# Forty unread products on TensorE around the first counts of a graph-layer kernel

## The chip, the cores and the metric

The kernel runs on one core of a Trainium2 chip. The core has five engines that run their own instruction streams and meet at semaphores: TensorE (PE, matrix products, with PEld for its weight loads), VectorE (DVE), ScalarE (ACT), GpSimd (POOL) and SyncE (SP, which issues transfers). The metric is the device time of one execution in microseconds. The time of a kernel is the median of several executions.

## The reference

One layer of a graph network over 6250 nodes with 64 features and 206250 edges sorted by destination:

```python
h = jnp.maximum(_layernorm(x, axis=-1), 0.0)
msg = h[src] + edge_attr_64
agg = jax.ops.segment_sum(msg, dst, num_segments=6250)
x = x + (jax.nn.relu(agg @ W1 + b1) @ W2 + b2)
```

## The kernel before

The 6250 nodes are 49 tiles of 128, handled as 25 double tiles of 256 (DTS = 25, LAST = 24; the last is half empty). The gather h[src] is not done row by row. For each double tile the kernel builds a table of counts, how often each source node feeds each destination node of the double tile, and multiplies it by h. So per double tile there are these steps:

- *Slots.* POOL gathers for each destination node up to 64 edge codes from a table in memory (gather_slots, L509, tile ell). The address comes from row pointers that DVE works out (L647), and those need another gather of POOL (gather_rows, L489, tile g).
- *Match and turn.* DVE marks foreign slots (match, L661, tile hi_m). PE transposes the codes (turn_codes, L805 and L806), ACT copies them out of PSUM (codes, L372).
- *Hots.* DVE writes one-hot tables lo_hot and hi_hot from the codes, in five batches (hots, L675), into two buffers. A batch waits until the counts of the batch two before it are done.
- *Counts.* PE multiplies lo_hot by hi_hot, 50 or 52 small products for each batch, in three thirds (count, L831). ACT copies each third from PSUM into the table (copy_counts, L407). A third waits for the copy of the third three before it.
- *Sums.* h is held as three bf16 parts. PE multiplies the table by two parts at once (high_sums, L844, 49 products of 256 columns) and by the third (low_sums, L852, 49 products), and adds the edge features with small f32 products (edge_sums, L866). All land in one PSUM bank, sum_ps.
- *Layer.* The sums go through W1, relu and W2 (hidden L881, rows L888), DVE adds x, SP stores.

PE's order is written out by hand. In pass j of its loop it runs rounds v = 0 to 4; in each it does batch v of the counts of double tile j, then a part of the sums of double tile m = j - 1, and at v = 2 the transposes for double tile j + 1 and turn_rel (L816, positions of edges) for j. HIGH and LOW say which part of the sums a round takes:

```python
HIGH = [0, 20, 20, 40, 40, 49]
LOW = [0, 0, 5, 5, 17, 49]
```

So pass 0 has counts and transposes alone, with nothing to sum yet. The first sums, 20 of them, stand behind the counts of batch 0 of pass 1. They wait for all copies of double tile 0. DVE and POOL run ahead of PE: at the time of pass 1's third round DVE matches double tile 2, whose slots POOL gathered before.

Of the kernel before, what the change touches and what calls it, by code (L numbers as in the profile page):

```python
# [6 lines left out]
def build_gnn_layer(nc, x, src, dst, edge, w1, b1, w2, b2, out):  # L7
# [6 lines left out]
    P = 128  # L14
# [45 lines left out]
    def steps_of(j):  # L60
        return 3 * batches_of(j)

    def step_index(j, u):
        return STEPS * j + u
# [10 lines left out]
    def tiles_in(j):  # L75
        return 2 if j < LAST else 1
# [11 lines left out]
    with ctx:  # L88
        def sb(name, shape, dt=f32):
            return ctx.enter_context(nc.sbuf_tensor(name, shape, dt))  # L90

        def ps(name, shape, dt=f32):
            return ctx.enter_context(nc.psum_tensor(name, shape, dt))

        def sem(name):
            return ctx.enter_context(nc.semaphore(name))
# [62 lines left out]
        ones_b = sb("ones_b", [P, P], bf16)  # L159
# [3 lines left out]
        ident_b = sb("ident_b", [P, P], bf16)  # L163
# [30 lines left out]
        sum_ps = [ps(f"sum_ps{b}", [P, 512]) for b in range(2)]  # L194
# [4 lines left out]
        def out_ps(f):  # L199
            return sum_ps[f % 2][:, 2 * P:2 * P + 2 * F]  # L200
# [4 lines left out]
        def rel_ps(j):  # L205
            return sum_ps[j % 2][:, 0:KK * 2 * CK]
# [26 lines left out]
        matched, turned, codes_made = sem("matched"), sem("turned"), sem("codes_made")  # L233
# [14 lines left out]
        with nc.Block() as block:  # L248
# [538 lines left out]
            def _(pe):  # L787
                pe.wait_ge(first_made, 1)
                for k in range(PR):
                    nc.tensor.matmul(row_ps, l_hot[:, k * P:(k + 1) * P], a_eq[:, k * HI:k * HI + NT],  # L790
                                     start=(k == 0), stop=False, skip_group_check=True)
                for k in range(PR):
                    last = nc.tensor.matmul(row_ps, ones_b[0:ROWP, :], a_lt[:, k * HI:k * HI + NT],
                                            start=False, stop=(k == PR - 1), skip_group_check=True)
# [13 lines left out]
                def turn_rel(j):  # L808
                    n = tiles_in(j) * CK
                    pe.wait_ge(rel_made, j + 1)  # L810
                    if j >= 1:
                        pe.wait_ge(rel_copied, j)
                    if j >= 2:
                        pe.wait_ge(rows_added, j - 1)
                    for k in range(KK):
                        last = nc.tensor.transpose(rel_ps(j)[:, k * 2 * CK:k * 2 * CK + n],  # L816
                                                   rel_rows[j % 2][0:n, k:CHUNK:KK], ident[0:n, 0:n])
                    last.then_inc(rel_turned, 1)

                def count(j, u):  # L820
                    g = step_index(j, u)
                    n = batch_index(j, u // 3)
                    if u % 3 == 0:
                        pe.wait_ge(hots_made, n + 1)
                    if g >= 3:
                        pe.wait_ge(copied, g - 2)
                    a, b = step_pairs(j, u)
                    for i in range(b - a):
                        for h in range(2):
                            rows = slice(h * SLOTS, (h + 1) * SLOTS)  # L830
                            last = nc.tensor.matmul(count_ps[u % 3][:, h, i * NT:(i + 1) * NT],  # L831
                                                    lo_hot[n % 2][rows, a + i, :], hi_hot[n % 2][rows, a + i, 0:NT],
                                                    start=True, stop=True)
                    last.then_inc(counted, 1)
# [6 lines left out]
                def high_sums(m, his):  # L841
                    cols = sum_cols(m)
                    for s in his:
                        nc.tensor.matmul(sum_ps[m % 2][:, 0:cols], parts[:, s, 0:2 * F],  # L844
                                         counts[m % 2][:, s, 0:cols], start=(s == 0), stop=False,
                                         skip_group_check=True)
# [29 lines left out]
                def hidden(f):  # L876
                    cols = 2 * P if f < LAST else 2 * HALF
                    pe.wait_ge(agg_copied, f + 1)
                    if f >= 1:
                        pe.wait_ge(rows_added, f)  # L880
                    nc.tensor.matmul(hid_ps(f)[:, 0:cols], w1_sb[:, :], agg_sb[:, 0:cols],  # L881
                                     start=True, stop=True).then_inc(hid_made, 1)

                def rows(f):
                    pe.wait_ge(relu_made, f + 1)
                    for h in range(tiles_in(f)):
                        n = P if f < LAST else NLAST
                        last = nc.tensor.matmul(out_ps(f)[0:n, h * F:(h + 1) * F], hid_sb[:, h * P:h * P + n], w2_sb[:, :],  # L888
                                                start=True, stop=True)
                    last.then_inc(rows_made, 1)  # L890

                HIGH = [0, 20, 20, 40, 40, 49]
                LOW = [0, 0, 5, 5, 17, 49]
                assert HIGH[-1] == NT and LOW[-1] == NT

                turn_codes(0)
                for j in range(DTS + 1):
                    m, f = j - 1, j - 2
                    for v in range(ROUNDS):
                        for u in range(3 * v, 3 * v + 3):  # L900
                            if j < DTS and u < steps_of(j):
                                count(j, u)
                        if f >= 0 and v == 0:
                            if f == 0:
                                pe.wait_ge(w_in, 80)
                            hidden(f)
                        if f >= 0 and v == 1:
                            rows(f)
                        if m >= 0:
                            if v == 0:  # L910
                                pe.wait_ge(copied, step_index(m, 0) + steps_of(m))
                                pe.wait_ge(rel_copied, m + 1)
                                pe.wait_ge(codes_made, min(m + 2, DTS))
                                if m == 0:
                                    pe.wait_ge(part_made, 2)
                                    pe.wait_ge(rest_in_parts, 1)
                                if m >= 2:
                                    pe.wait_ge(agg_copied, m - 1)
                                if m == LAST - 2:
                                    pe.wait_ge(shift_made, 1)  # L920
                                if m == LAST:
                                    pe.wait_ge(far_read, 1)
                            high_sums(m, range(HIGH[v], HIGH[v + 1]))
                            if v % 2 == 1 and v // 2 < tiles_in(m):
                                edge_sums(m, v // 2, range(TILES_E))
                            if LOW[v] < LOW[v + 1]:
                                last = low_sums(m, range(LOW[v], LOW[v + 1]))
                            if v == ROUNDS - 1:
                                last.then_inc(sums_done, 1)
                        if v == 2 and j + 1 < DTS:  # L930
                            turn_codes(j + 1)
                        if v == 2 and j < DTS:
                            turn_rel(j)
                        if j == LAST - 2 and v == 3:
                            pe.wait_ge(rp_made, DTS)
                            pe.wait_ge(codes_made, LAST)
                            pe.wait_ge(rel_copied, LAST - 1)
                            nc.tensor.matmul(shift_ps[0:P - HALF, :], ident[:, HALF:P], rp_f[:, NT - 1:NT],
                                             start=True, stop=True).then_inc(shifted, 1)
                        if j == LAST and v == 3:  # L940
                            pe.wait_ge(r0_set, LAST)
                            pe.wait_ge(rel_copied, DTS)
                            nc.tensor.matmul(next_ps, next_a, rp_f[:, 0:NT], start=True, stop=False)
                            nc.tensor.matmul(next_ps, next_b, rp_f[:, 1:NT + 1], start=False, stop=True)
                            nc.tensor.matmul(base_ps, ones[0:1, 0:P], r0_f[0:1, :], start=True, stop=True
                                             ).then_inc(far_found, 1)
                        if j == DTS and v == 2:
                            pe.wait_ge(worst_made, 1)
                            pe.wait_ge(rows_added, DTS - 1)
                            nc.tensor.transpose(worst_ps[0:1, :], worst[:, 0:1], ident).then_inc(worst_turned, 1)  # L950
# [167 lines left out]
```

## Time and profile before

| | us |
|---|---|
| median of 3 runs | 521.38 |
| lowest, highest | 519.58, 523.01 |
| the profiled execution | 519.95 |
| its span, first to last instruction | 518.2 |

| engine | busy us | share of the span | instructions |
|---|---|---|---|
| PE | 459.3 | 89% | 12541 |
| PEld | 405.9 | 78% | 12541 |
| DVE | 435.2 | 84% | 531 |
| ACT | 380.2 | 73% | 481 |
| POOL | 322.5 | 62% | 223 |

How to read it: the busy share is an average over stages. The first 50 us build tables and have little work for PE. The page also gives the TensorE clock granted over the span, on average 0.992 of full speed. The chain of waits follows the work that ended last back from the end, each step to what released it. A group of instructions in a timeline is merged, and a pause ahead of it stands in brackets with its releaser.

### The profile page before, as it was taken

The page shows a single profiled execution, that of the slowest core. Times are in us where ns is not written, and L with a number is a line of the kernel's source. Part 1 is how long each engine was busy: PE and PEld are TensorE (multiplying, and loading weights), DVE is VectorE, ACT ScalarE, POOL GpSimd, SP SyncE. Part 2 cuts the span into 40 slices and gives each one's busy share as a digit, 9 for nine tenths or more (in the row PEclk, how much of TensorE's full clock was granted, in tenths as well). Part 3 has the DMA queues.
Part 4 walks back from the last instruction along what each step waited for, and adds up shares of the span by engine and source line. Part 5 has one row for each costly group of instructions (what it writes and reads, how often), then busy time and mean ns, then how long its engine had stood idle before and what let it go on. Part 6 is the DMA issues. An engine that isn't in the chain of part 4 may idle for free.

```text
span 518.2 us, 27591 instructions
## 1 busy us (share of the span) xinstructions
PE 459.3 (89%) x12541; PEld 405.9 (78%) x12541; DVE 435.2 (84%) x531; ACT 380.2 (73%) x481; POOL 322.5 (62%) x223
## 2 busy tenths in 40 slices
PE   1012799999999999999999999999999999999994
PEld 1002688898889888888888988988898898888883
DVE  4989977988988998998898899889889988969550
ACT  2846766787878787787878878878787887878720
POOL 4379998976676566657756666756757675125200
PEclk9999989999999999999999999999999999999997
DMA  9758057643663474466357346536744643661200
GB/s 203 186 142 259 19 145 198 203 133 111 185 187 103 141 200 121 114 187 171 97 159 201 107 126 193 150 94 178 195 108 130 198 131 99 185 182 51 78 3 10
DMA packets 139626, 73.65 MB, mean 142 GB/s; under 512 B 23644, under 2 KB 137550, under 8 KB 139382
## 3 DMA queue, kind: packets, MB, share of 16 engines
q1 hardware_dynamic: 136105, 65.30, 45.8%
q0 software_dynamic: 3168, 4.90, 3.5%
q8 instruction: 100, 1.64, 1.2%
q10 hardware_dynamic: 234, 1.65, 1.0%
q14 instruction: 19, 0.16, 0.1%
HBM read 66.98 MB, written 4.86 MB: 139 GB/s over the span
## 4 chain that ended last, share of the span: by engine, by line
PE 84%; POOL 6%; DMA 3%; ACT 2%; DVE 2%; issue 1%; SPq 0%; ACTq 0%; DVEq 0%; POOLq 0%
PE sum_ps L844 25%; PE sum_ps L866 21%; PE count_ps L831 17%; PE sum_ps L852 14%; POOL ell L509 3%; PE sum_ps L881 3%; PE sum_ps L888 3%; POOL g L489 2%; DMA comb_rows<-counts 1%; PE sum_ps L816 1%; DMA dst_sb<-in_dst 1%; DMA ell<-comb_rows,ell_idx 1%; ACT counts L343 1%; ACT counts L345 1%; POOL r_f L496 1%
## 5 line engine op out<-in xcount | busy, mean ns | idle before, releaser
L407 ACT CAST counts<-count_ps 128x882 bf16<-128x882 f32 (+2 forms) x369 | 327.0, 978 | 60.2 <-PE count_ps L831 59.1
L675 DVE TENSOR_TENSOR lo_hot<-iota_lo,codes 128x3328 bf16<-128x3328 bf16 (+3 forms) x123 | 229.9, 1869 | 41.3 <-PE count_ps L831 25.0
L509 POOL DMA_INDIRECT ell<-comb_rows,ell_idx x50 | 105.2, 2103 | 90.2 <-DVE ell_idx L647 56.5
L844 PE MATMUL sum_ps<-counts,h_parts 128*128 128x256 bf16 (+1 forms) x1225 | 145.4, 273 | 0.0
L844 PEld LDWEIGHTS sum_ps<-counts,h_parts 128*128 128x128 bf16 x1225 | 114.5, 99 | 18.2
L831 PE MATMUL count_ps<-hi_hot,lo_hot 64*128 64x49 bf16 x6256 | 110.4, 183 | 16.8 <-DVE hi_hot L675 14.8
L831 PEld LDWEIGHTS count_ps<-hi_hot,lo_hot 64*128 64x128 bf16 x6256 | 96.0, 94 | 37.3 <-DVE hi_hot L675 19.6
L489 POOL DMA_INDIRECT g<-in_dst,row_i x49 | 95.5, 1949 | 37.9 <-DVE e_hot L689 21.3
L866 PE MATMUL sum_ps<-e_hot,edges 128*64 128x24 f32 x3528 | 112.9, 217 | 1.0 <-issue 1.0
L866 PEld LDWEIGHTS sum_ps<-e_hot,edges 128*64 128x64 f32 x3528 | 107.7, 138 | 3.7 <-issue 1.1
L675 DVE TENSOR_TENSOR hi_hot<-iota_hi,codes 128x1300 bf16<-128x1300 bf16 (+3 forms) x123 | 103.9, 844 | 0.0
L852 PE MATMUL sum_ps<-counts,h_parts 128*64 128x256 bf16 (+1 forms) x1225 | 81.1, 273 | 0.3 <-issue 0.3
L852 PEld LDWEIGHTS sum_ps<-counts,h_parts 128*64 128x64 bf16 x1225 | 62.0, 111 | 6.1 <-issue 5.7
L520 POOL TENSOR_SCALAR rel_rows<-dst_rows,tile_base 36x256 f32<-36x256 int32 (+1 forms) x25 | 47.7, 1910 | 24.3 <-DMA dst_rows<-in_dst 23.4
L689 DVE TENSOR_TENSOR e_hot<-win_tab,rel_sb 128x864 f32<-128x864 f32 x49 | 53.0, 1081 | 5.7 <-ACT rel_sb L381 5.7
L390 ACT COPY agg_sb<-sum_ps 128x256 f32<-128x256 f32 (+1 forms) x25 | 9.2, 367 | 36.3 <-PE sum_ps L852 36.3
L528 POOL TENSOR_TENSOR x_sb<-x_sb,b_all 128x128 f32<-128x128 f32 (+1 forms) x25 | 28.2, 1130 | 1.6
L805 PE MATMUL sum_ps<-ident_b,ell 128*128 128x128 bf16 x25 | 5.6, 224 | 21.7 <-DVE hi_m L661 21.7
L499 POOL CAST r_i<-r_f 1x2 int32<-1x2 f32 x24 | 22.9, 954 | 1.5
L805 PEld LDWEIGHTS sum_ps<-ident_b,ell 128*128 128x128 bf16 x25 | 2.8, 113 | 22.2 <-issue 19.3
L496 POOL TENSOR_SCALAR r_f<-rp_f 1x2 f32<-1x2 f32 x24 | 17.3, 722 | 2.5 <-DVE rp_f L649 1.9
L372 ACT COPY codes<-sum_ps 128x512 bf16<-128x512 bf16 x25 | 14.8, 593 | 5.4 <-PE sum_ps L806 5.4
(107 smaller groups left out, 213.7 us busy)
## 6 DMA issues: line engine op xcount, KB each, us to landing
edges<-in_edge_attr SPq DMA_DIRECT2D x98, 576.0 KB, 5.2
h_rows<-h_sb SPq DMA_DIRECT2D x1, 1568.0 KB, 10.3
x_sb<-in_x SPq DMA_DIRECT2D x4, 384.0 KB, 10.2
out<-o_sb SPq DMA_DIRECT2D x24, 64.0 KB, 1.7
comb_rows<-counts ACTq DMA_DIRECT2D x1, 1443.8 KB
dst_rows<-in_dst SPq DMA_DIRECT2D x49, 18.0 KB
ell<-comb_rows,ell_idx POOLq DMA_INDIRECT x50
g<-in_dst,row_i POOLq DMA_INDIRECT x49, 4.0
```

The lines of the kernel that those rows point to most:

```text
L407: nc.scalar.copy(counts[j % 2][:, :, 0:2 * half].rearrange("p s (h i) -> p h s i", h=2)[:, :, :, first + a:first + b], count_ps[u % 3][:, ...
L489: nc.gpsimd.indirect_dma_start(out=g2[j % 2][:, h, :], out_offset=None, in_=dst.rearrange("(r e) -> r e", e=STEP), in_offset=bass.Indirect ...
L499: nc.gpsimd.tensor_copy(r0_i[0:1, 2 * j:2 * j + n], r0_f[0:1, 2 * j:2 * j + n]).then_inc(r0_made, 1)
L509: nc.gpsimd.indirect_dma_start(out=ell[j % 2][0:rows, h, :, :].rearrange("p s w -> p (s w)"), out_offset=None, in_=comb_dram[:, :], in_off ...
L520: nc.gpsimd.tensor_scalar(rel_rows[j % 2][0:n * CK, :], dst_rows[j % 2][0:n * CK, :], float(2 * j * P), tile_base[0:n * CK, 0:1], ALU.subt ...
L528: nc.gpsimd.tensor_tensor(x_sb[:, tiles, :], x_sb[:, tiles, :], bc(b2_all[:, :].rearrange("p (o f) -> p o f", o=1), [P, tiles_in(f), F]), ...
L675: return nc.vector.tensor_tensor(out_ap.rearrange("p i (a t) -> p i a t", t=2), bc(table_ap.rearrange("p (o a t) -> p o a t", o=1, t=2), [ ...
L689: nc.vector.tensor_tensor(e_hot[h][:, :, :].rearrange("p (c k) w -> p c k w", k=KK), bc(win_tab[:, m // LAST, :, :].rearrange("p c (o w) - ...
L831: last = nc.tensor.matmul(count_ps[u % 3][:, h, i * NT:(i + 1) * NT], lo_hot[n % 2][rows, a + i, :], hi_hot[n % 2][rows, a + i, 0:NT], sta ...
L844: nc.tensor.matmul(sum_ps[m % 2][:, 0:cols], parts[:, s, 0:2 * F], counts[m % 2][:, s, 0:cols], start=(s == 0), stop=False, skip_group_che ...
L852: last = nc.tensor.matmul(sum_ps[m % 2][half, 0:cols], parts[:, s, 2 * F:3 * F], counts[m % 2][:, s, 0:cols], start=False, stop=False, ski ...
L866: last = nc.tensor.matmul(sum_ps[m % 2][half, low:low + W], edges[t % SLOT_EDGES][:, c, k * F:(k + 1) * F], e_hot[h][:, i, :], start=False ...
```

## The change

A helper keep_busy issues a number of products of the identity (ident_b, the weights) with a table of ones (ones_b, 128 columns) into the first 128 columns of sum_ps[1]. Nobody reads them. The next user of this bank starts with start=True. In pass 0 ten such products follow the work of each of the rounds 2, 3 and 4, behind a wait for codes_made of at least 1 (ACT's copy of double tile 0's codes, which read the same bank). In pass 1 ten more stand in round 0, between the counts and the first sums. All other engines' instructions stay as they were.

```diff
+                def keep_busy(times):
+                    for _ in range(times):
+                        nc.tensor.matmul(sum_ps[1][:, 0:P], ident_b[:, :], ones_b[:, :], start=True, stop=True)
+
                 HIGH = [0, 20, 20, 40, 40, 49]
                 LOW = [0, 0, 5, 5, 17, 49]
                 assert HIGH[-1] == NT and LOW[-1] == NT
@@ -906,6 +910,8 @@
                             hidden(f)
                         if f >= 0 and v == 1:
                             rows(f)
+                        if j == 1 and v == 0:
+                            keep_busy(10)
                         if m >= 0:
                             if v == 0:
                                 pe.wait_ge(copied, step_index(m, 0) + steps_of(m))
@@ -931,6 +937,9 @@
                             turn_codes(j + 1)
                         if v == 2 and j < DTS:
                             turn_rel(j)
+                        if j == 0 and v >= 2:
+                            pe.wait_ge(codes_made, 1)
+                            keep_busy(10)
```

PE's order before, from the transposes of pass 0 to the first sums of pass 1 (count_ps0 to count_ps2 are the three thirds of a batch, and hi_hot0 and hi_hot1 the two buffers of hots):

```order
L816 MATMUL sum_ps0<-wide,rel_rows0 128x36 x2
L831 MATMUL count_ps0<-hi_hot1,lo_hot1 128x49 x18
L831 MATMUL count_ps1<-hi_hot1,lo_hot1 128x49 x16
L831 MATMUL count_ps2<-hi_hot1,lo_hot1 128x49 x16
L831 MATMUL count_ps0<-hi_hot0,lo_hot0 128x49 x18
L831 MATMUL count_ps1<-hi_hot0,lo_hot0 128x49 x16
L831 MATMUL count_ps2<-hi_hot0,lo_hot0 128x49 x16
L831 MATMUL count_ps0<-hi_hot1,lo_hot1 128x49 x18
L831 MATMUL count_ps1<-hi_hot1,lo_hot1 128x49 x18
L831 MATMUL count_ps2<-hi_hot1,lo_hot1 128x49 x16
L844 MATMUL sum_ps0<-counts0,h_parts 128x256 x20
```

The same place in the changed kernel, from the transposes to the second group of new products (L894 is the new line):

```order
L816 MATMUL sum_ps0<-wide,rel_rows0 128x36 x2
L894 MATMUL sum_ps1<-ones_b,ident_b 128x128 x10
L831 MATMUL count_ps0<-hi_hot1,lo_hot1 128x49 x18
L831 MATMUL count_ps1<-hi_hot1,lo_hot1 128x49 x16
L831 MATMUL count_ps2<-hi_hot1,lo_hot1 128x49 x16
L894 MATMUL sum_ps1<-ones_b,ident_b 128x128 x10
```

And from there, behind the last counts of pass 0, to the first sums of pass 1:

```order
L831 MATMUL count_ps2<-hi_hot0,lo_hot0 128x49 x16
L894 MATMUL sum_ps1<-ones_b,ident_b 128x128 x10
L831 MATMUL count_ps0<-hi_hot1,lo_hot1 128x49 x18
L831 MATMUL count_ps1<-hi_hot1,lo_hot1 128x49 x18
L831 MATMUL count_ps2<-hi_hot1,lo_hot1 128x49 x16
L894 MATMUL sum_ps1<-ones_b,ident_b 128x128 x10
L844 MATMUL sum_ps0<-counts0,h_parts 128x256 x20
```

Nothing changed its place among the old instructions; four groups of ten stand between them, one ahead of each of the three batches of counts and one ahead of the sums.

## Rows read from the trace of the kernel before

**Rows 1.** The page, chain that ended last: shares of the span by engine.
```profile
PE 84%; POOL 6%; DMA 3%; ACT 2%; DVE 2%; issue 1%; SPq 0%; ACTq 0%; DVEq 0%; POOLq 0%
```

**Rows 2.** Chain of waits, 26 to 85 us: start, duration, what.
```profile
50.13 12.38 POOL ell L509
...
62.81 4.54 DMA ell<-comb_rows,ell_idx
...
69.74 0.73 DVE hi_hot L675
```

**Rows 3.** PE's waits, 49 to 79.4 us, then 79.4 to 490: total, times, longest.
```profile
PE count_ps L831 <- DVE hi_hot L675: 4.6, 4, 1.8
```
```profile
PE count_ps L831 <- issue: 1.4, 2, 0.9
```

**Rows 4.** Timeline of PE, 0 to 80 us: start, duration, instructions, pause before.
```profile
49.78 0.45 PE L816 MATMUL sum_ps<-wide,rel_rows 36*128 36x36 f32 x2
52.05 1.22 PE L831 MATMUL count_ps<-hi_hot,lo_hot 64*128 64x49 bf16 x50 [1.82 <-DVE hi_hot L675]
54.51 0.89 PE L831 MATMUL count_ps<-hi_hot,lo_hot 64*128 64x49 bf16 x34 [1.23 <-DVE hi_hot L675]
55.87 0.52 PE L831 MATMUL count_ps<-hi_hot,lo_hot 64*128 64x49 bf16 x16 [0.47 <-ACT counts L407]
57.06 1.58 PE L831 MATMUL count_ps<-hi_hot,lo_hot 64*128 64x49 bf16 x52 [0.67 <-DVE hi_hot L675]
58.57 4.18 PE L844 MATMUL sum_ps<-counts,h_parts 128*128 128x256 bf16 x20
62.68 0.84 PE L831 MATMUL count_ps<-hi_hot,lo_hot 64*128 64x49 bf16 x52
...
66.76 2.36 PE L844 MATMUL sum_ps<-counts,h_parts 128*128 128x256 bf16 x20
...
69.16 0.43 PE L816 MATMUL sum_ps<-wide,rel_rows 36*128 36x36 f32 x2
70.52 0.81 PE L831 MATMUL count_ps<-hi_hot,lo_hot 64*128 64x49 bf16 x50 [0.93 <-DVE hi_hot L675]
71.26 2.98 PE L866 MATMUL sum_ps<-e_hot,edges 128*64 128x24 f32 x72
...
79.35 0.81 PE L831 MATMUL count_ps<-hi_hot,lo_hot 64*128 64x49 bf16 x50
```

**Rows 5.** Timeline of all engines, 30 to 80 us, rows of ACT and DVE.
```profile
52.65 8.02 ACT L407 CAST counts<-count_ps 128x882 bf16<-128x882 f32 x9 [0.50 <-PE count_ps L831]
...
61.93 1.88 DVE L675 TENSOR_TENSOR lo_hot<-iota_lo,codes 128x3328 bf16<-128x3328 bf16 x1
...
67.38 0.48 DVE L661 SCALAR_TENSOR_TENSOR hi_m<-ell,node_f 128x64 bf16<-128x64 f32 x2 [2.82 <-DMA ell<-comb_rows,ell_idx]
...
67.92 1.82 DVE L675 TENSOR_TENSOR lo_hot<-iota_lo,codes 128x3200 bf16<-128x3200 bf16 x1
```

**Rows 6.** Busy time by microsecond; the third number from the end is PE's clock.
```profile
72.00:73.00 1.00, 1.00 (x36) 1.00 (x32) 1.00 (x3) 1.00 (x3) 1.00 (x1) 0.79 0.37 108
73.00:74.00 1.00, 1.00 (x24) 1.00 (x24) 1.00 (x1) 1.00 (x2) 1.00 (x1) 0.50 0.00 1
...
76.00:77.00 1.00, 1.00 (x40) 0.90 (x35) 0.85 (x2) 0.94 (x2) 1.00 (x1) 1.00 0.61 170
...
86.00:87.00 1.00, 0.43 (x15) 0.42 (x16) 0.01 (x1) 0.00 (x0) 0.95 (x1) 1.00 0.36 82
```

**Rows 7.** Timeline of PE, 76 to 200 us.
```profile
86.57 1.18 PE L866 MATMUL sum_ps<-e_hot,edges 128*64 128x24 f32 x35 [1.05 <-issue]
...
128.74 0.22 PE L831 MATMUL count_ps<-hi_hot,lo_hot 64*128 64x49 bf16 x2
...
129.72 2.29 PE L866 MATMUL sum_ps<-e_hot,edges 128*64 128x24 f32 x72
...
136.31 0.84 PE L831 MATMUL count_ps<-hi_hot,lo_hot 64*128 64x49 bf16 x52
```

## The prediction

> **What bounds the kernel now.** I read the page's chain shares first: TensorE (PE) holds 84% of the chain that ended last, POOL 6% and DMA 3% [rows 1]. So PE is the bound over most of the span, but not everywhere, and the change sits in the part where I must know which. The second view is the chain of waits around the edit, 50 to 71 us. There it does not run on PE. It runs through a POOL gather of slots that takes 12.38 us from 50.13, the landing of that double tile's gathers (4.54 us from 62.81) and then DVE's match and one-hots, the last of which ends at 70.47 [rows 2]. Only after that, with the counts at 70.52, does the chain enter PE. The third view is PE's waits: from 49 to 79.4 us it waited 4.6 us for DVE's hi_hot; from 79.4 to 490 us it waited for no engine at all, the largest entry being 1.4 us of "issue" [rows 3]. The reader is to see two regimes: up to 70.5 us PE is fed late by POOL, DMA and DVE and has slack; from 70.5 us on every microsecond that PE loses or wins stays to the end.
>
> The fourth view is PE's timeline through the edit [rows 4]. Counts of 50 or 52 products take 1.22 to 1.26 us at first, 0.81 to 0.84 later. The first 20 high sums take 4.18 us at 58.57, the next 20 take 2.36 us at 66.76. That is a factor of nearly two on the same shapes, so PE ran at 1.2 GHz until about 62.5 us and at 2.4 GHz after. (The granted-clock column reads 1.00 there already; I go by the durations.) Later the column does show a fall: 0.79 in the microsecond from 72, 0.50 from 73, 1.00 again from 76 [rows 6]. If the fraction of the first is split between the two levels, the clock fell at 72.6. Ahead of that fall PE had stood still for 0.93 us, from 69.59 to 70.52, waiting for hi_hot [rows 4].
>
> **What the change adds.** Forty products of 128x128 by 128 columns in four groups of ten, each with its weight load: one group after the transposes of double tile 0's round 2, one after its round 3, one after its round 4, and one between the first counts of double tile 1 and the first sums. Nothing is removed or moved. The three groups in double tile 0 wait for codes_made of 1, and ACT had to raise that before any hot could be made, long ago; these waits are free.
>
> Price of one product: half of a 256-column sum. At 1.2 GHz 4.18 us over 20 is 209 ns, so 105 ns each and 1.05 us a group. At 2.4 GHz 2.36 us over 20 is 118 ns, so 59 ns each and 0.59 us a group [rows 4]. All forty cost 2.4 to 4.2 us of PE. The Trainium skill, in "TensorE: Matmul & The Clock Gate", section "Wait — 56ns, not 53.3ns?", has 107 and 56 ns for this width, and by it the forty would cost 2.2 to 4.3 us; the trace agrees within 6%.
>
> Where they lie, at the dear price. *Group 1* starts when the transposes end at 50.23 and ends at 51.28; the next counts began at 52.05, released by DVE: hidden. *Group 2* starts at 53.27 and ends at 54.32; the next counts began at 54.51: hidden, with 0.2 us to spare. *Group 3* starts at 56.39 and ends at 57.44; counts began at 57.06, so they are 0.38 us late. These 52 counts took 1.58 us to the sums' start, where others of 52 take 1.26, since the last third waited for ACT's copy. Without a pause they now end at 57.44 + 1.26 = 58.7 instead of 58.57. *Group 4* is uncovered: 1.05 us, so the sums start at 59.8 instead of 58.57 [rows 4]. Who would notice? Behind these products on PE stand the counts, and DVE waits for the counts two batches back before it refills a buffer. Its lo_hot at 61.93 and 67.92 need counts that ended at 58.57 and 63.5: each has over 3 us of margin, and DVE shows no idle before the 2.82 us in which it waits for the gathered slots at 67.38 [rows 5]. ACT copies without a gap from 52.65 to 60.67, nine copies, so the last of them, which takes the late counts, starts only near 59.8 [rows 5]. So nothing on the POOL, DMA and DVE chain moves. If the cover were gone, all forty would cost 2.4 to 4.2 us.
>
> What they bring. PE works more continuously from 50 to 59 us, and the clock can rise sooner than at 62.5. At best it is at 2.4 GHz when the sums start. Then they take 2.36 us instead of 4.18, the fourth group costs 0.59, and PE is done with the sums 4.18 - 2.36 - 0.59 = 1.2 us ahead of before. If the clock rises no sooner than before, (62.5 - 59.8) / 0.209 = 13 sums run slowly, the other 7 take 0.83, and PE is done at 63.35, 0.6 us later than before (62.75).
>
> **Where that goes.** Both end at the counts of 70.52. They need DVE's hi_hot, ready at 70.47, and PE was at that point at 69.59. PE 0.6 us later: still 0.3 us in time. PE 1.2 us earlier: it first waits for match at 67.86 to do the transposes, then for 70.47 [rows 2, 4, 5]. Direct term: 0 from both sides. The one term left is the clock with which PE goes into the stretch from 70.52, where it is the bound. From the counts at 70.52 to the first counts of the next double tile at 79.35 it took 8.83 us; the same stretch three double tiles on takes 7.57 us (128.74 to 136.31) at 2.4 GHz [rows 4, 7]. So the fall of 72.6 costs 1.26 us now. The changed kernel has it, has more of it, or has none of it. PE stands still between 69.59 and 70.52 now; after an early rise it would stand still for longer, up to 0.9 + 1.2 = 2.1 us. The only fall in the trace inside the work came right after such a pause, so the fall should stay, and may come sooner. Price of sooner: the counts of 70.52 at 1.22 instead of 0.81 us (0.41), and the edge sums. Their 72 products from 71.26 took 2.98 us with the fall inside [rows 4]. At the rate of the clean stretch (2.29 us for 72, 32 ns each [rows 7]) some 42 were done in the 1.34 us to 72.6, and the other 30 took 1.64 us, 55 ns each; all at 55 ns is 3.96, or 0.98 more. Together +1.4 us. I take 0 for this term as the likeliest, with ends of -1.26 and +1.4.
>
> The sum: profiled execution 519.95 us + 0 + 0 = 519.95. It lies 1.43 us under the median of the three runs, 521.38, whose span (519.58 to 523.01) is as wide as the ends of my term; so **521.4 us** for the median.
>
> A rule bears on this. The rows give the cold stretch as 57 to 62.5 us, some 1% of the span, and it cannot give more than half of that back, 2.8 us. The Trainium skill, same page, section "What's actually happening", says that the slow start costs under 1% of a typical kernel, and that the number of slow products at its start differs from run to run. By that rule too this change can't be measured at the 1% bound, and the rule says besides that one profile is no proof of where the clock rises.
>
> **Rivals.**
> 1. *The half clock comes sooner after the longer pause*: slower, the other side. Place: PE's counts and edge sums from 70.5; price +1.4 us, 522.8. It decides if PE's granted clock is at 0.50 when hi_hot lands. For: the fall of 72.6 followed a pause of 0.93 us, which the change can double. Against: PE also stood still for 1.05 us ahead of 86.57 ("issue") [rows 7] with no fall in the microsecond after [rows 6]. Chance 0.2.
> 2. *The fall goes away*: -1.26 us, 520.1. For: it came only once within the work, and what PE does before it moves. Against: the pause gets longer. Chance 0.15.
> 3. *The early gain goes through in full*, because the chain is on PE there after all: -1.2 us, 520.2. Against: the 0.93 us wait at 70.52 would have to be misread. Chance 0.03.
> 4. *The change doesn't do what it says*: the clock rises no sooner, and the fourth group delays the sums. The 0.6 us is within the slack, 521.4. Chance 0.1.
> 5. *Something larger*, such as the 12.38 us gather coming out another way: over 5.2 us either way. No row leads there from these products. Chance 0.05.
>
> **How the numbers follow.** The forecast (clock sooner, time the same) has the rest, 0.47. One per cent is 5.2 us, about what a measurement can tell from no change; cases 1 to 4 and the forecast all lie within it. Of case 5 I give 0.02 to faster and 0.03 to slower. The range takes the ends of the clock term (520.1 and 522.8) and some 1.1 us more on either side, since the median of before moved by 1.8 and 1.6 us between runs: 519.0 to 523.9. About 2 in 10 is left out.
>
> **What would show it.** Right: in the profile of the changed kernel the first 20 sums take 2.2 to 3 us instead of 4.18, PE's wait for hi_hot ahead of the counts near 70.5 grows from 0.93 to about 2 us, and those counts start within 0.3 us of 70.52. Wrong in the cover: DVE's hots or POOL's gather start later than at 61.93 and 62.81. Wrong in the clock term: the stretch from these counts to the next double tile's takes 7.6 us (fall gone) or 10.2 us (fall sooner) instead of 8.8. The whole prediction is wrong if the counts near 70.5 move by over 1 us, since then PE or the products touch the POOL and DVE chain.

## The result and the profile after

| | before | changed |
|---|---|---|
| median of 6 runs, us | 521.51 | 535.77 |
| lowest, highest | 519.58, 523.01 | 533.78, 538.62 |
| profiled execution | 519.95 | 538.62 |
| its span | 518.2 | 536.9 |

The changed kernel is slower by 2.8%: ratio 1.0279, 95% interval 1.0255 to 1.0303. The forecast of 521.4 us and its range of 519.0 to 523.9 missed it. Medians in this document are of all executions, ratios only of those within 1.5% of the fastest execution of the same kernel, so that a ratio can differ from the quotient of two medians.

Where PE's idle time went, from the view of waits of the changed kernel (line, waited for: us in total, times, longest):

```profile
PE count_ps L831 <- DVE hi_hot L675: 11.0, 5, 4.6
...
PE sum_ps L844 <- issue: 6.3, 4, 2.2
PE sum_ps L852 <- issue: 5.1, 8, 1.2
PE count_ps L831 <- issue: 4.6, 3, 2.0
...
PE sum_ps L866 <- issue: 0.3, 1, 0.3
```

"Issue" is idle time in which PE waited for no engine that the profile shows. It is 16.3 us here; before it was 2.7 us behind 79.4 us, with 1.4 us as the largest entry [rows 3].

PE's timeline of the changed kernel (start, duration, instructions, pause before) shows that this does not happen where the products were put, but later:

```profile
58.05 1.25 PE L894 MATMUL sum_ps<-ones_b,ident_b 128*128 128x128 bf16 x10
59.10 2.70 PE L844 MATMUL sum_ps<-counts,h_parts 128*128 128x256 bf16 x20
...
69.06 0.81 PE L831 MATMUL count_ps<-hi_hot,lo_hot 64*128 64x49 bf16 x50 [0.22 <-DVE hi_hot L675]
...
77.62 0.70 PE L881 MATMUL sum_ps<-agg_sb,w_sb 128*128 128x256 f32 x2
...
86.85 0.24 PE L831 MATMUL count_ps<-hi_hot,lo_hot 64*128 64x49 bf16 x5 [1.72 <-issue]
87.02 4.02 PE L844 MATMUL sum_ps<-counts,h_parts 128*128 128x256 bf16 x20
...
245.36 1.14 PE L852 MATMUL sum_ps<-counts,h_parts 128*64 128x256 bf16 x17 [0.45 <-issue]
...
321.67 1.58 PE L852 MATMUL sum_ps<-counts,h_parts 128*64 128x256 bf16 x25 [1.20 <-issue]
340.74 1.69 PE L852 MATMUL sum_ps<-counts,h_parts 128*64 128x256 bf16 x27 [0.66 <-issue]
...
437.44 0.70 PE L844 MATMUL sum_ps<-counts,h_parts 128*128 128x256 bf16 x5 [1.71 <-issue]
457.87 0.93 PE L844 MATMUL sum_ps<-counts,h_parts 128*128 128x256 bf16 x7 [2.24 <-issue]
...
529.13 0.47 PE L881 MATMUL sum_ps<-agg_sb,w_sb 128*128 128x112 f32 x2 [0.35 <-ACT agg_sb L390]
```

The first product with W1 (L881) stands at 77.62, where before it stood at 80.12:

```profile
80.12 0.70 PE L881 MATMUL sum_ps<-agg_sb,w_sb 128*128 128x256 f32 x2
...
510.29 0.47 PE L881 MATMUL sum_ps<-agg_sb,w_sb 128*128 128x112 f32 x2 [0.35 <-ACT agg_sb L390]
```

So at the end of the first double tile the changed kernel was 2.5 us ahead. The products in place are not what brought that: with 20 products far ahead of them and none in place (e6 below) the first L881 stands at 77.67 too. From the first to the last L881 the changed kernel took 451.5 us instead of 430.2: 21.3 us lost, all in the steady part, where both kernels have the same instructions. Pauses of kind issue are 13.3 us of it (16.0 in the changed kernel behind 77 us, 2.7 before). Three of them, of 1.72, 2.24 and 2.02 us, each go with a fall of PE's clock to 1.2 GHz at or soon after their end. For the first, the busy time by microsecond shows it (the third number from the end is the clock):

```profile
87.00:88.00 1.00, 1.00 (x10) 0.70 (x6) 0.80 (x1) 0.81 (x1) 0.97 (x2) 0.55 0.18 52
88.00:89.00 1.00, 1.00 (x7) 0.71 (x5) 1.00 (x2) 0.00 (x0) 1.00 (x1) 0.50 0.31 91
```

Twenty high sums took 4.02 us there instead of 2.36 [rows 4], 1.7 us more; three times that, some 5 us, is my estimate for the three falls. The other 3 us I can't book to single rows; low sums of 2.34 us instead of 1.94 behind 133 us are of that kind.

The rows also show a pattern. At each pause PE stands a given number of products short of the end of a group: 17, 25, 27 low sums, later 5, 7 high sums. That number grows by two per double tile. This looks as if something were counted off in PE's instruction stream.

**The theory, F.** PE's instructions come from memory in blocks. The page of the kernel before has them as a DMA queue (packets, MB, share of the engines):

```profile
q8 instruction: 100, 1.64, 1.2%
```

That is 100 transfers of 16 KB for 12541 products and as many weight loads, some 65 bytes an instruction, so some 250 instructions in a block. The pattern above fits 256, or 128 products with their loads. A double tile has 508 such products by PE's timeline, and the trace has 300 separate waits of PE, 12 for each of the 25 double tiles: 1028 instructions, four more than four blocks. So block ends fall two products earlier in each double tile, which the rows show. The Trainium skill has such a mechanism ("Runtime: NRT & Kernel Launch", section "Instruction fetch mechanics"): the engine's sequencer fetches blocks of 256 instructions by its own queue while it runs the current one, and the cost of a block's end is "mostly hidden". The size agrees with the trace; that it is hidden does not.

The transfers around the pause that ends at 245.36, in the changed kernel (queue, packets, MB, share of the engines), from 242.9 to 243.1 us:

```profile
q1 hardware_dynamic: 102, 0.05, 82.6%
q8 instruction: 1, 0.02, 29.2%
```

and SyncE's timeline ahead of it:

```profile
237.60 5.04 SPq L279 DMA_DIRECT2D edges<-in_edge_attr  x4
```

The block's transfer started only when the issue of the edge transfers was through (242.64), at 242.97, took 0.93 us by the trace's record of transfers, and PE went on 1.46 us after it had landed. I took the same difference for all 52 pauses of 0.4 us or more in six kernels (both given ones, e5 to e8): PE goes on 1.23 to 1.58 us after the last instruction block landed. In 37 of the 52 the block's transfer started within 0.9 us of the end of the edge transfer that SyncE had issued last. In the other 15, all those ahead of 90 us among them, it did not, and what those blocks queued behind is not shown. The kernel before had the same conflict (edges issued from 237.25 to 243.36, the block's transfer within 243.5 to 243.7) and got by, since its block ended 40 products later. When PE asks for a block is in no record. But the trace of e13, which has e5's products and small edge transfers, shows when blocks start to come where nothing holds them up. PE passes the products of e5's 21 pauses there too, and in 18 cases the next block's transfer starts 0.1 to 1.2 us after that; in the other three one starts 0.2 to 0.6 us ahead of it. So a block seems to be asked for when PE enters the one before it, as that section of the Trainium skill says.

**The rival, C.** The products in place change PE's clock or its idle time around the first sums, and the loss grows out of that.

### The profile page after: what moved, and what is told of

It is laid out like the page before. It is cut to its first block, busy times and chain, and to the rows that moved or that the text cites. A ratio compares the mean times of both kernels' runs of the same rounds, so it can differ in the third digit from the quotient of the medians.

```text
span 536.9 us, 27671 instructions
## 1 busy us (share of the span) xinstructions
PE 468.9 (87%) x12581; PEld 410.5 (76%) x12581; DVE 435.7 (81%) x531; ACT 380.8 (71%) x481; POOL 275.4 (51%) x223
## 4 chain that ended last, share of the span: by engine, by line
PE 85%; DVE 8%; issue 4%; DMA 1%; ACT 1%; SPq 0%; DVEq 0%
PE sum_ps L844 26%; PE sum_ps L866 20%; PE count_ps L831 17%; PE sum_ps L852 14%; PE sum_ps L881 3%; PE sum_ps L888 3%; DVE lo_hot L675 1%; PE sum_ps L816 1%; DMA dst_sb<-in_dst 1%; DVE h_sb L572 1%; DVE hi_hot L675 1%; DVE mean L570 1%; DVE h_sb L585 1%; DVE counts L600 1%; DVE var L578 1%
## 5 line engine op out<-in xcount | busy, mean ns | idle before, releaser
L844 PE MATMUL sum_ps<-counts,h_parts 128*128 128x256 bf16 (+1 forms) x1225 | 147.2, 274 | 6.3 <-issue 6.3
L509 POOL DMA_INDIRECT ell<-comb_rows,ell_idx x50 | 85.5, 1709 | 103.3 <-DVE ell_idx L647 65.6
L489 POOL DMA_INDIRECT g<-in_dst,row_i x49 | 90.1, 1839 | 54.4 <-DVE e_hot L689 39.7
L675 DVE TENSOR_TENSOR hi_hot<-iota_hi,codes 128x1300 bf16<-128x1300 bf16 (+3 forms) x123 | 105.5, 858 | 0.0
L852 PE MATMUL sum_ps<-counts,h_parts 128*64 128x256 bf16 (+1 forms) x1225 | 85.0, 276 | 5.3 <-issue 5.1
L520 POOL TENSOR_SCALAR rel_rows<-dst_rows,tile_base 36x256 f32<-36x256 int32 (+1 forms) x25 | 32.4, 1294 | 57.0 <-DMA dst_rows<-in_dst 56.8
L528 POOL TENSOR_TENSOR x_sb<-x_sb,b_all 128x128 f32<-128x128 f32 (+1 forms) x25 | 34.8, 1395 | 1.6
L381 ACT COPY rel_sb<-sum_ps 128x72 f32<-128x72 f32 (+1 forms) x25 | 5.7, 227 | 18.8 <-PE sum_ps L816 18.8
L881 PE MATMUL sum_ps<-agg_sb,w_sb 128*128 128x256 f32 (+1 forms) x50 | 17.3, 427 | 0.8 <-ACT agg_sb L390 0.8
```

The costliest lines, as they stand in the source:

```text
L489: nc.gpsimd.indirect_dma_start(out=g2[j % 2][:, h, :], out_offset=None, in_=dst.rearrange("(r e) -> r e", e=STEP), in_offset=bass.Indirect ...
L509: nc.gpsimd.indirect_dma_start(out=ell[j % 2][0:rows, h, :, :].rearrange("p s w -> p (s w)"), out_offset=None, in_=comb_dram[:, :], in_off ...
L520: nc.gpsimd.tensor_scalar(rel_rows[j % 2][0:n * CK, :], dst_rows[j % 2][0:n * CK, :], float(2 * j * P), tile_base[0:n * CK, 0:1], ALU.subt ...
L528: nc.gpsimd.tensor_tensor(x_sb[:, tiles, :], x_sb[:, tiles, :], bc(b2_all[:, :].rearrange("p (o f) -> p o f", o=1), [P, tiles_in(f), F]), ...
L675: return nc.vector.tensor_tensor(out_ap.rearrange("p i (a t) -> p i a t", t=2), bc(table_ap.rearrange("p (o a t) -> p o a t", o=1, t=2), [ ...
L852: last = nc.tensor.matmul(sum_ps[m % 2][half, 0:cols], parts[:, s, 2 * F:3 * F], counts[m % 2][:, s, 0:cols], start=False, stop=False, ski ...
```

## The experiments

All shifts use the change's own helper. "Early" products stand ahead of the first transposes, where PE had 19 us with nothing to do:

```diff
+                keep_busy(N)
                 turn_codes(0)
```

The runs were measured in four groups, each on a chip of its own and together with the kernel before. Two of the chips were restless: the kernel before itself took 526 to 544 us beside e1 to e4 and 531 to 550 us beside e9 to e12, against 520 to 526 us beside e5 to e8 and 520 to 524 us beside e13 to e16. So times of different groups can't be compared, only ratios to before of the same group.

| run | in place | early | shift of block ends | median us | ratio to before (95%) | PE's issue pauses, us |
|---|---|---|---|---|---|---|
| e8 | 0 | 0 | 0 | 522.0 | 0.9995 (0.9964, 1.0025) | 2.9 |
| e12 | 0 | 10 | 10 | 535.5 | 0.9956 (0.9839, 1.0074) | 5.8 |
| e6 | 0 | 20 | 20 | 519.0 | 0.9932 (0.9892, 0.9971) | 3.9 |
| e10 | 20 | 0 | 20 | 531.1 | 0.9918 (0.9830, 1.0005) | 5.5 |
| e14 | 20 | 0 | 20 | 518.8 | 0.9959 (0.9930, 0.9988) | 4.4 |
| e11 | 40 | 108 | 128 + 20 | 528.6 | 0.9871 (0.9781, 0.9961) | 5.0 |
| the change | 40 | 0 | 40 | 535.8 | 1.0279 (1.0255, 1.0303) | 16.3 |
| e1 | 0 | 40 | 40 | 545.3 | 1.0280 (1.0158, 1.0403) | 17.2 |
| e5 | 0 | 64 | 64 | 563.6 | 1.0786 (1.0688, 1.0883) | 35.5 |
| e7 | 0 | 108 | 108 | 535.6 | 1.0266 (1.0211, 1.0321) | 11.2 |
| e3 | 0 | 128 | 128 | 537.7 | 1.0107 (0.9967, 1.0247) | 11.0 |
| e15 | 0 | 128 | 128 | 521.8 | 0.9998 (0.9976, 1.0020) | 5.9 |
| e2 | 40 | 88 | 128 | 540.0 | 1.0176 (1.0044, 1.0308) | 11.8 |
| e9 | 40 | 88 | 128 | 541.7 | 1.0016 (0.9884, 1.0148) | 8.9 |
| e16 | 40 | 88 | 128 | 521.7 | 0.9995 (0.9968, 1.0021) | 7.4 |
| e4, few edges | 40 | 0 | 40 | 525.8 | 0.9911 (0.9868, 0.9955) | 0.9 |
| e13, few edges | 0 | 64 | 64 | 514.8 | 0.9869 (0.9849, 0.9890) | 1.6 |

**e1, all forty early.**

> The forty unread products stand in one group ahead of the first transposes, where PE of the kernel before has 19 us with nothing to do; none stand around the first sums. Everything behind them has the same place in PE's instruction stream as in the changed kernel. Theory F (instruction fetch): PE's instructions come in blocks of 16 KB (256 instructions, 128 products with their weight loads), the next block is fetched by a transfer of queue q8 that can queue behind the edge transfers, and PE stands still when it reaches the end of a block too early. What costs time is where the ends of the blocks fall, so this kernel must be as slow as the changed one: 533 to 538 us, with pauses of kind issue on PE of 14 to 18 us in all, growing from double tile to double tile behind 240 us in low sums and high sums. Theory C (the clock): what costs time is that PE works more between 50 and 59 us, its clock or its pauses behind that; then this kernel has the time of before, 520 to 523 us.

Measured: ratio 1.028, that of the change, with 17.2 us of pauses, 9.8 us of them in low and high sums, nearly all behind 240 us. Nothing stands around the sums in this kernel. The time, 545.3 us, is over both expectations, as before took 534.4 us beside it. The sign speaks for F, but this group can't decide: e2 and e3, which F wants at the time of before, came out at 1.018 and 1.011 in it, and their intervals overlap that of e1. C falls by the quiet chips: e5 has nothing near the sums and is 7.9% slower, and e16 has the change's forty in place and is not slower at all.

**e2, e9 and e16, a whole block.** The change, and 88 early.

> The changed kernel with its forty products in place, and 88 more unread products ahead of the first transposes: 128 in all, just one block of 256 instructions. Theory F: from the first sums on every end of a block falls where it fell in the kernel before, one block later. So the pauses of kind issue behind 75 us are back to the 2.7 us of before and the time is 519.5 to 522 us, although more is added than by the change. Theory C: the products around the sums are still there, so 533 to 538 us, or more.

The 540.0 us and the 11.8 us of pauses missed what F expects; taken alone they are on the side of C. But before took 534.4 us beside it. The second and third try:

> The kernel of e2 once more (the change's forty products in place and 88 ahead of the first transposes, one whole block of instructions in all), since in its call the kernel before itself ran from 526 to 544 us. Theory F: if the chip is as quiet as that of e5 to e8, the time is within 1% of before, 518 to 526 us, with pauses of kind issue on PE of under 5 us behind 75 us. A theory by which the products around the sums cost by themselves wants 530 us or more.

> The kernel of e2 and e9 a third time (the change's forty in place and 88 early), which came out at 1.018 and 1.002 with wide intervals. Theory F: ratio 0.993 to 1.005, the same as e15 within 0.5%. If it is over e15 by 1% or more, the products around the sums, or the clock that they raise, cost something of their own.

The time of e9 missed too (541.7 us, pauses 8.9 us), on a restless chip where before had 541.7 us; its ratio was 1.002. e16 settles it: ratio 0.9995, though it adds 128 products where the change adds 40. A whole block gives the time back. The pauses did not go back to 2.7 us, as e2's expectation had it, but to 7.4 us. That e2 had 1.0176, with 1 outside its interval, on the same edit stays unexplained.

**e3 and e15, a whole block, all of it early.**

> The kernel before with 128 unread products (one whole block of instructions) ahead of the first transposes and none later. It shows what early products cost by themselves. Both theories: 520 to 523 us, as before. If it is slower than 525 us, early products cost something of their own and the first two runs must be read with that.

> The kernel of e3 once more (a whole block of products, all early), whose interval was 0.997 to 1.025 on a restless chip. Theory F: ratio 0.995 to 1.005.

e3 came out at 537.7 us, over the expected 520 to 523, with before at 534.4; e15 at ratio 0.9998. Early products by themselves cost nothing that can be measured. And e16 against e15 prices the forty products in place by themselves: 521.71 to 521.82 us, nothing within intervals of some 1.3 us to either side. Their pauses stand at the same products, in PE's timelines of e15 and of e16:

```profile
103.70 0.33 PE L831 MATMUL count_ps<-hi_hot,lo_hot 64*128 64x49 bf16 x13 [1.48 <-issue]
```

```profile
103.40 0.34 PE L831 MATMUL count_ps<-hi_hot,lo_hot 64*128 64x49 bf16 x13 [1.48 <-issue]
```

In the kernel before the pause of that double tile stands 13 products short of the counts' end too:

```profile
100.33 0.35 PE L831 MATMUL count_ps<-hi_hot,lo_hot 64*128 64x49 bf16 x13 [0.88 <-issue]
```

Two more pauses of e15 and e16, ahead of 81 us, are not in the first profile of the kernel before but in its second one, e8. So which of its block ends are late changes from one execution to the next.

**e5, half a block early.**

> The kernel before with 64 unread products (half a block of instructions) ahead of the first transposes, none later. Theory F says where the next block's end falls against the edge transfers. Before, about double tile 10, PE crossed into a block at about 241.3 us, inside the edge transfers of 237.3 to 243.4, the next block's transfer started only at 243.6, when they were issued, and its instructions were there near 245.9; PE needed them at 246.2, just in time. 64 products earlier is some 2.3 us earlier, so PE stands still for some 2 us in each of 24 double tiles: 25 to 60 us more than before in the same call. Theory C (the clock, or work near the sums) says no change.

Measured: 563.6 us against 521.9, 41.8 us more, with 35.5 us of pauses. From its waits, and one pause of its timeline:

```profile
PE count_ps L831 <- issue: 26.8, 13, 2.4
PE sum_ps L844 <- issue: 5.9, 4, 2.2
PE sum_ps L852 <- issue: 2.8, 4, 1.0
```

```profile
294.89 0.22 PE L831 MATMUL count_ps<-hi_hot,lo_hot 64*128 64x49 bf16 x3 [2.09 <-issue]
```

**e6, e7 and e8: the edges of the good region, and before again.**

> The kernel before with 20 unread products ahead of the first transposes. Theory F: block ends 20 products earlier, half the shift of the change, so the pauses start later in the kernel (behind 340 us instead of 240) and the time is 2 to 9 us over before of the same call. Theory C: as before, within 0.5%.

> The kernel before with 108 unread products ahead of the first transposes, that is one block less 20 products, so that block ends fall 20 products later in the program than before. Theory F: the late end of the good region; the pauses of before behind 85 and 100 us move, and the time is within 1.5% of before, either sign, clearly under the run with 64. Theory C, or a theory by which more early products cost more, wants it at or above the run with 64.

> The kernel before, unchanged, with a profile on the same chip as the other runs of this call: ratio 1.00. Its pauses of kind issue are what the others' are to be held against. In the first call the kernel before took 526 to 544 us; if this chip too is slower than the 521 us of the record, theory F wants the excess in pauses of kind issue.

e6 missed its expectation on the good side: 2.9 us under before. Late pauses do come (0.43 to 0.93 us, four of them behind 420 us), and the early ones are fewer. Before again, and then e6, from their timelines ahead of 90 us:

```profile
74.78 0.76 PE L831 MATMUL count_ps<-hi_hot,lo_hot 64*128 64x49 bf16 x46 [1.12 <-issue]
...
80.86 0.33 PE L831 MATMUL count_ps<-hi_hot,lo_hot 64*128 64x49 bf16 x12 [1.75 <-issue]
```

```profile
88.21 0.70 PE L844 MATMUL sum_ps<-counts,h_parts 128*128 128x256 bf16 x5 [1.25 <-issue]
```

The pauses don't explain the gain, since e6 has more of them in all (3.9 us against 2.9). Nor do the profiled executions show it: e6's took 519.82 us, that of e8 518.76. They differ in one fall of the clock, at 82.02 us in e8 and none in e6 ahead of 515 us. Why e6 is faster in the median stays open.

e7 missed on the bad side: 2.7% slower where I expected 1.5% at most, with pauses such as this, all before 230 us:

```profile
121.06 0.55 PE L831 MATMUL count_ps<-hi_hot,lo_hot 64*128 64x49 bf16 x29 [2.80 <-issue]
```

So of a circle of 128 products the good places are narrow: of the shifts tried, 0 and 20 are good, 10 probably (its interval holds 1, on a restless chip), 40, 64 and 108 bad.

**e4 and e13, few edges.** PE's instructions as in the change and as in e5, but from the third double tile on each edge transfer loads one chunk instead of nine, so that the sums use stale edge features:

```diff
+                    n = CK // 2 if t < SLOT_EDGES else 1
                     for c in range(0, CK, CK // 2):
-                        sp.dma_start(edges[t % SLOT_EDGES][:, c:c + CK // 2, :],
-                                     edge[bass.ds(first + c * CHUNK, RANGE // 2), :].rearrange(
+                        sp.dma_start(edges[t % SLOT_EDGES][:, c:c + n, :],
+                                     edge[bass.ds(first + c * CHUNK, n * CHUNK), :].rearrange(
```

> The changed kernel, but from the third double tile on each edge transfer loads one chunk of 256 edges instead of nine, so the sums are formed with stale edge features; all instructions of PE stay as they are. Theory F, with the fetch late because it queues behind the edge transfers: the pauses of kind issue of 16 us fall under 3 us, and the time is 515 to 521 us. If the fetch is late by itself (a fixed latency, no contention) they stay at 14 us or more and the time at 532 us or more. Theory C has no reason for a gain from this: 533 to 538 us.

> The kernel of e5 (64 unread products ahead of the first transposes, the slowest place found for block ends), but from the third double tile on each edge transfer loads one chunk instead of nine, so the sums are formed with stale edge features; PE's instructions are those of e5. Theory F with the instruction transfers queuing behind the edge transfers: the 35 us of pauses of kind issue in e5 fall under 4 us and the time is at or under before of the same call (ratio 0.98 to 1.00). If the block end by itself is what costs, whatever else the DMA engines do, it stays 30 us or more over before.

e4 took 525.8 us (over the expected 521, but before took 534.4 beside it), 19 us under e1 with the same block ends. e13 took 514.8 us, 1.3% under before, where e5 took 7.9% more. The only PE pauses of kind issue left in e13 (L832 is the counts' line there):

```profile
PE count_ps L832 <- issue: 1.6, 2, 1.2
```

So the place of the block ends costs time nearly only together with the edge transfers. Nearly: the 1.2 us of e13 stand at the same product, at 86 us, as pauses of 2.37 us in e5 and 1.72 us in the change, and the block's transfer started there some 10 us after SyncE's last edge transfer was issued. What is in the way there is not shown.

**e10, e11, e12 and e14: can one gain by it?** Groups of five instead of ten; the change with 108 early; ten early.

> The change with groups of five products instead of ten: twenty in all, in the same four places. Theory F: block ends stand as in e6, so 517 to 520.5 us, at or a little under e6's ratio of 0.993, and faster than both given kernels. If the places of the products matter and not their number, it must be nearer to the change, 525 us or more.

> The change's forty products in place and 108 ahead of the first transposes: 148, one whole block and 20 products. Theory F: the same block ends as e6 and e10, 517 to 522 us, though 3.7 times as many products are added as by the change. Else 535 us or more.

> The kernel before with 10 unread products ahead of the first transposes. Theory F has the good places for block ends between a shift of 0 (pauses of 2.7 to 2.9 us) and of 20 (3.9 us, clock falls fewer), so 517.5 to 521.5 us, ratio 0.99 to 1.00.

> The kernel of e10 once more (the change with groups of five), since before took 531 to 550 us in that call. Theory F: ratio 0.985 to 0.997; the clock at the first sums is up as in the change, which adds nothing that e6 (0.993) does not have, since PE waits for DVE behind them anyway.

The times of e10, e11 and e12 were over their numbers, but before had 541.7 us beside them; the ratios are 0.992, 0.987 and 0.996. e14, on a quiet chip, is at 518.8 us against 522.0, ratio 0.9959 (0.9930 to 0.9988). Groups of five beat the kernel before by 0.4%, and with it the change. But e6, with twenty products early and none near the sums, has 0.9932, so the gain goes with the shift by twenty and needs no product at the sums. What in the shift brings it is not shown: as with e6, the profiled execution of e14 (520.46 us) is no shorter than that of e8.

## Why the prediction was wrong

- *The early part was right in its direct term.* The first 20 sums took 2.70 us, within the 2.2 to 3 that I named, and forty products in place cost and gain nothing (e16 against e15: 0.1 us). It was right for the reason given: PE is not the bound before 70 us. The details were off. The wait for hi_hot shrank to 0.22 us instead of growing to 2, and the counts came at 69.06 and not at 70.52. That is over the 1 us that I had named as the sign that the whole prediction is wrong, because the products touch the chain of POOL and DVE. The sign was badly chosen. The changed kernel's profile was 0.66 us early already at the transposes ahead of the first new product (48.79 against 49.45). From there to these counts it took 20.27 us, as in e1 and e15, which have no product at the sums (20.27 both); the first profile of the kernel before took 21.06, its second (e8) 20.41. So this time moves by itself from one execution to the next.
- *The clock term was small, as said, but came out as rival 2 and not as forecast.* The fall of 72.6 [rows 6] is gone in the changed kernel: from the counts at 69.06 to the next double tile's at 76.86 it took 7.8 us, near the 7.6 named for that. That need not be the products' doing: e8, which is the kernel before once more, has no fall there either (its fall comes at 82.02). The other falls of the changed kernel come behind pauses that I had not forecast.
- *The step that failed* is "Nothing is removed or moved", and behind it "no row leads there from these products" in rival 5. The edit moved something: the place of each of some 90 block ends against the work and against the edge transfers, by 40 products of 128. The row for it was there. PE's largest wait from 79.4 to 490 us was "issue" [rows 3], and the pause ahead of 86.57 stood in the middle of a run of edge products, with no group to wait for [rows 7]. I used it only as evidence on the clock. I had also said that each of the forty products brings its weight load, 80 instructions in all, and priced them by their time on the array alone. The term that I left at 0 measures 13.3 us of pauses and, by estimate, some 5 us of slow clock in the profiled execution, which is 18.7 us longer; the medians are 14.3 us apart.
- *Sums.* They come out as written, but for the 1.58 us "to the sums' start": that is the counts' duration, and from start to start it is 1.51 us. Nothing hangs on it.
- *The range* was made from the ends of the clock term, 2.7 us wide, and run-to-run spread. The mechanism that decided was covered only by the 0.03 of rival 5 that lay on the slower side.
- *What stays open:* why some chips had 10 to 20 us more in all kernels (e3 on the restless chip has 11.0 us of pauses, e15, the same kernel, 5.9 us, and that is a third of the 16 us between them); what gives a shift of twenty its 0.4 to 0.7%; and what holds up the blocks ahead of 90 us.

## What to carry to other kernels

If a fully unrolled kernel has an engine that eats many short instructions, look in its timeline for pauses of kind issue in the middle of a run of equal instructions, and count the products from one to the next: a constant number, or one that drifts by a few per loop, is the instruction stream and not the work. Then any edit that adds or removes instructions ahead of the steady part, even free ones, moves all later block ends, and is best judged at two or three shifts before its own effect is believed. To test it, put the same number of instructions into an idle stretch, and then fill up to a whole block.

## What the runs showed of the hardware

- An instruction block that falls into the edge transfers can make PE stand still for some 2 us, as e5 against e13 shows (35.5 us of pauses against 1.6). Over a circle of 128 products the time of this kernel ran from 519 to 564 us, 8.6%, with unread products alone added.
- PE goes on 1.23 to 1.58 us after the late block's landing, in 52 of 52 pauses of 0.4 us or more on the quiet chips. On the restless one some pauses are of another kind: 0.49 us at 108.48 in e1 ended 1.99 us after a landing, 0.50 us at 87.11 in e3 0.21 us after one.
- In the same six kernels 19 pauses lasted 1.7 us or more, and 8 of them went with a fall of PE's clock to 1.2 GHz (three of four in the changed kernel, three of 13 in e5), so a late block can cost twice.
- One edit (e2, e9, e16) gave ratios of 1.0176, 1.0016 and 0.9995. On the two restless chips its interval was 0.026 wide, on the quiet one 0.005: a single measurement on a restless chip should not decide a per cent.
